# Edge softmax of a graph layer on one Trainium2 core: one pair of scans for two, and an accumulator cleared and added up by two engines

## What is computed

```python
alpha = einsum('ehc,hc->eh', leaky_relu(x_r[dst] + x_j, 0.2), att) + log(edge_attr)[:, None]   # 8 heads
amax  = segment_max(alpha, dst)
ex    = exp(alpha - amax[dst])
denom = segment_sum(ex, dst)
out   = segment_sum(x_j * (ex / denom[dst])[..., None], dst)
```

## Time and profile before

| what | time |
|---|---|
| median of the timed runs | 5361.09 us |
| span of the profiled execution (the profile gives no other time of it) | 5935.3 us |
| `normalise_edges`, first to last instruction of VectorE | 1488.2 to 1611.0 us |
| `aggregate_edges`, first to last instruction of VectorE | 1612.0 to 2075.7 us |
| last addition (L1109) | 13.74 us |

### The profile page before, as it was taken

How to read it: one execution, slowest core, us unless ns; L and a number is a source line. 1 busy time by engine, 2 the same in 40 slices (tenths; PEclk the granted TensorE clock), 3 DMA queues, 4 the chain that set the end, 5 groups by cost and what they waited for, 6 DMA issues and landing times. The chain is left out here.

```text
span 5935.3 us, 66919 instructions
## 1 busy us (share of the span) xinstructions
PE 3546.3 (60%) x13782; PEld 2710.2 (46%) x13783; DVE 2982.8 (50%) x6982; ACT 1018.9 (17%) x2146; POOL 3055.9 (51%) x2888
## 2 busy tenths in 40 slices
PE   4744455454389865998444544454445454466998
PEld 3633233232267654776433433333434444455666
DVE  5466566666899964445433333334333333354443
ACT  0111121121179801221000000000000000013121
POOL 1266677676368624221466666663666666612111
PEclk9877767776599976998566566655555555566999
DMA  4487666666578762223311111111111111123221
GB/s 108 136 217 211 202 207 203 204 206 195 158 227 271 224 188 88 63 63 97 106 28 28 29 28 28 29 29 32 28 29 28 28 29 28 29 62 98 70 87 37
DMA packets 432122, 617.01 MB, mean 104 GB/s; under 512 B 100329, under 2 KB 309161, under 8 KB 431721
## 3 DMA queue, kind: packets, MB, share of 16 engines
q1 hardware_dynamic: 304733, 389.03, 21.1%
q0 software_dynamic: 107440, 200.97, 14.1%
q10 hardware_dynamic: 19852, 25.94, 1.6%
HBM read 419.67 MB, written 209.64 MB: 106 GB/s over the span
## 5 line engine op out<-in xcount | busy, mean ns | idle before, releaser
L1857 POOL DMA_INDIRECT big<-t_d,src_tiles x1564 | 1483.7, 949 | 957.2 <-issue 450.8
L2080 PE MATMUL v_bank<-big,v_oh 128*128 x3328 | 716.2, 390 | 1216.6 <-issue 830.3
L2080 PEld LDWEIGHTS v_bank<-big,v_oh 128*128 128x128 f32 x3328 | 674.7, 300 | 1302.8 <-issue 1302.2
L653 POOL DMA_INDIRECT big<-xl_d,src_steps x832 | 859.8, 1033 | 378.1 <-issue 356.0
L1935 DVE TENSOR_TENSOR big<-big,v_bank 128x64 f32 x1664 | 366.5, 220 | 1285.3 <-DMA xj_d<-big 973.2
L759 PE MATMUL se_z_ps<-big,se_oht 128*128 x1664 | 608.7, 517 | 628.5 <-issue 385.9
L759 PEld LDWEIGHTS se_z_ps<-big,se_oht 128*128 128x128 f32 x1664 | 386.8, 250 | 850.4 <-issue 780.7
L692 DVE TENSOR_TENSOR se_z<-se_z_ps,big 128x528 f32<-128x528 f32 x416 | 291.4, 700 | 461.1 <-DMA es_ts<-src_p 256.8
L1122 PE MATMUL ae_bank<-ae_v,ae_oh 128*128 128x266 f32 x1664 | 402.3, 397 | 49.8 <-DVE big L1106 36.7
L1081 POOL TENSOR_TENSOR ae_v<-ae_v,ex 128x1792 f32<-128x1792 f32 x104 | 334.1, 3215 | 178.1 <-DMA ae_v<-xj_d 178.0
L1122 PEld LDWEIGHTS ae_bank<-ae_v,ae_oh 128*128 128x128 f32 x1664 | 310.4, 191 | 141.5 <-DVE big L1106 53.0
(11 more groups left out here) (468 smaller groups left out, 5316.9 us busy)
## 6 DMA issues: line engine op xcount, KB each, us to landing
xj_d<-big SPq DMA_DIRECT2D x208, 528.0 KB
ae_v<-xj_d SPq DMA_DIRECT2D x208, 528.0 KB
se_dlb<-dlr_d SPq DMA_DIRECT2D x104, 256.0 KB
big<-t_d,src_tiles POOLq DMA_INDIRECT x1564
buf_d<-ne_blank SPq DMA_DIRECT2D x4, 4112.0 KB
e_xs<-buf_d SPq DMA_DIRECT2D x106, 129.0 KB, 2.1
big<-xl_d,src_steps POOLq DMA_INDIRECT x832
cp_y<-y_d SPq DMA_DIRECT2D x14, 896.0 KB, 7.4
```

The lines of the kernel that those rows point to most:

```text
L653: nc.gpsimd.indirect_dma_start(half_of(u)[:, k, :], None, table, bass.IndirectOffsetOnAxis(ap=m.src[:, t:t + 1], axis=0)).then_inc(landed[ ...
L1857: nc.gpsimd.indirect_dma_start(rows[:, t % RING, :], None, table, bass.IndirectOffsetOnAxis(ap=m.srct[:, t:t + 1], axis=0)).then_inc(lande ...
L2080: last = nc.tensor.matmul(bank[u][:, k * MH:(k + 1) * MH], oh[:, u, k, :], of_block(rows, at[k]), start=True, stop=True)
```

## The change

In `normalise_edges`:

- One forward scan inside the chunks and one backward scan over its result, both without initial value. Both ends of every chunk (`cols`, now four columns) then go through one merge, in which forwards and backwards lie side by side in rows of 256.
- Columns that belong to the chunk's first or last segment get the neighbours' maximum by two masks: `off_first` = (key - first key) * -1e30 in `m.ex`, `off_last` = (last key - key) * -1e30 in `key`. ScalarE makes both in four passes over 6656 columns, between its copies for the folding. VectorE applies each with `max(top, mask + carry)` in four quarters, ahead of the subtraction.
- L867 is cut into four quarters by step; the scaling of `run` (L861) moves behind them.
- On TensorE the transposes move ahead of the second product of the folding; ScalarE, not VectorE, copies their 13 groups out of PSUM. Of the 13 groups on the way back ScalarE copies 7 (between its exponentials), VectorE 6.

In `aggregate_edges`:

- GpSimd clears `acc` before its first multiplication; VectorE clears `acc1` as its second instruction, ahead of L1092 of group 0.
- The last addition is shared: blocks 0 to 30 on VectorE, 31 to 48 on GpSimd.

The core of the diff:

```diff
@@ normalise_edges, VectorE
+                c.did(V.tensor_copy(cols[:, 1:2], key[:, 0:1]))
+                c.did(V.tensor_copy(cols[:, 2:3], key[:, CL - 1:CL]))
+                c.did(V.tensor_scalar(minus[:, :], key[:, 0:1], -1.0, None, ALU.mult))
...
-                V.tensor_tensor(top.rearrange(...), exv, lnw..., ALU.add).then_inc(s["logw"], 1)
-                for q in range(NQ4):
-                    dve.wait_ge(s["turned"], q + 1)
-                    V.tensor_copy(al[:, q * 512:(q + 1) * 512], bank[q % 4][:, :]).then_inc(s["back"], 1)
+                for q in range(4):
+                    j = slice(q * J4, (q + 1) * J4)
+                    V.tensor_tensor(turned_top[:, :, j, :], exv[:, :, j, :], wide[:, :, j, :], ALU.add).then_inc(s["logw"], 1)
+                dve.wait_ge(s["same"], 1)
+                c.did(V.tensor_scalar(run[:, 1:CL], run[:, 1:CL], -1.0, -MASKED, ALU.add, ALU.mult))
                 dve.wait_ge(s["back"], NQ4)
...
+                c.did(V.tensor_tensor_scan(top, run[:, 0:CL], al, MASKED, ALU.add, ALU.max))
+                c.sync()
+                c.did(V.tensor_tensor_scan(top[:, ::-1], run[:, 1:CL + 1][:, ::-1], top[:, ::-1], MASKED, ALU.add, ALU.max))
+                c.sync()
+                V.tensor_copy(cols[:, 0:1], top[:, CL - 1:CL]).then_inc(s["cols"], 1)
+                V.tensor_copy(cols[:, 3:4], top[:, 0:1]).then_inc(s["cols"], 1)
...             (one merge: six copies of a row, the operations of L903 to L918 on 256 columns)
+                c.did(V.tensor_copy(carry[:, :], bank[1][:, 0:2]))
+                dve.wait_ge(s["apart"], 4)
+                for q in range(4 + 2):
+                    if q < 4:
+                        V.scalar_tensor_tensor(top[:, o], off_first[:, o], carry[:, 0:1], top[:, o], ALU.add, ALU.max).then_inc(s["left"], 1)
+                    if 0 <= q - 1 < 4:
+                        dve.wait_ge(s["left"], q)
+                        V.scalar_tensor_tensor(top[:, o], off_last[:, o], carry[:, 1:2], top[:, o], ALU.add, ALU.max).then_inc(s["right"], 1)
+                    if 0 <= q - 2:
+                        dve.wait_ge(s["right"], q - 1)
+                        V.tensor_tensor(al[:, o], al[:, o], top[:, o], ALU.subtract).then_inc(s["exps"], 1)
+                for q in range(ON_ACT, NQ4):      # ON_ACT = 7, NQ4 = 13
                     dve.wait_ge(s["unturned"], q + 1)
+                    V.tensor_copy(*unturned_out(q)).then_inc(s["done_dve"], 1)
@@ ScalarE, behind a_back
+                for q in range(NQ4):
+                    act.wait_ge(s["turned"], q + 1)
+                    nc.scalar.copy(al[:, q * 512:(q + 1) * 512], bank[q % 4][:, :]).then_inc(s["back"], 1)
+                nc.scalar.activation(off_first, key, ACT.Identity, bias=minus[:, 0:1], scale=1.0).then_inc(s["apart"], 1)
                 (kv_back)
+                nc.scalar.mul(off_first, off_first, MASKED).then_inc(s["apart"], 1)
                 (t1_back)
+                nc.scalar.activation(off_last, key, ACT.Identity, bias=cols[:, 2:3], scale=-1.0).then_inc(s["apart"], 1)
                 (m0_back x3)
+                nc.scalar.mul(off_last, off_last, MASKED).then_inc(s["apart"], 1)
+                exps(0); exps(1); copy_out(0..2); exps(2); copy_out(3..5); exps(3); copy_out(6)
@@ aggregate_edges
+                nc.gpsimd.memset(acc[:, :, :], 0.0).then_inc(s["cleared"], 1)          # GpSimd, ahead of its loop
+                pool.wait_ge(s["added"], NS)
+                nc.gpsimd.tensor_tensor(acc[:, ON_DVE:NB, :], acc[:, ON_DVE:NB, :], acc1[:, ON_DVE:NB, :], ALU.add)
+                V.memset(acc1[:, :, :], 0.0).then_inc(s["cleared"], 1)                 # VectorE, ahead of its loop
-                        V.memset(acc[:, :, :], 0.0).then_inc(s["zeroed"], 1)
-                        V.memset(acc1[:, :, :], 0.0).then_inc(s["zeroed"], 1)
-                        dve.wait_ge(s["zeroed"], 3)
+                        dve.wait_ge(s["cleared"], 2)
-                V.tensor_tensor(acc[:, :, :], acc[:, :, :], acc1[:, :, :], ALU.add)
+                V.tensor_tensor(acc[:, 0:ON_DVE, :], acc[:, 0:ON_DVE, :], acc1[:, 0:ON_DVE, :], ALU.add)   # ON_DVE = 31
```

More of the change, by code:

```diff
@@ L776, in normalise_edges @@
         small, lnw, empty = sb("small", [P, NS]), sb("lnw", [P, NS]), sb("empty", [P, NS])
-        cols = sb("cols", [P, 4])
-        cki, carry = sb("cki", [P, 1]), sb("carry", [P, 2])
-        rows = sb("rows", [1, 6, P])
+        cols, minus = sb("cols", [P, 4]), sb("minus", [P, 1])
+        carry = sb("carry", [P, 2])
+        rows = sb("rows", [1, 7, 2 * P])
         bank = [ctx.enter_context(nc.psum_tensor(f"ne_bank{i}", [P, 512], F32)) for i in range(4)]
         blank = sb("blank", [P, 1, RW])
-        s = {n: m.sem("ne_" + n) for n in "blank blanked w ln logw turned back cols rowps rows colps exps exped unturned done chain".split()}
+        s = {n: m.sem("ne_" + n) for n in ("blank blanked w ln ends same logw turned back apart cols rowps rows colps left right exps exped unturned "
+                                         "done_act done_dve chain").split()}
         wfct, wq, wkt, wvt = (sb(n, [P, KC, D]) for n in ("wfct", "wq", "wkt", "wvt"))
@@ L866, in _ @@
                 c.sync()
[L867 to L872 removed]
+                wide = lnw[:, :].rearrange("p (c j) -> p c j", c=CH).unsqueeze(3).to_broadcast([P, CH, CS, H])
@@ L875, in _ @@
                 c.sync()
[L877 to L886, removed]
@@ L887, in _ @@
-                c.sync()
[L888 to L922, removed]
@@ new lines, in _ @@
+                V.tensor_copy(cols[:, 0:1], top[:, CL - 1:CL]).then_inc(s["cols"], 1)
+                V.tensor_copy(cols[:, 3:4], top[:, 0:1]).then_inc(s["cols"], 1)
+                VALUE, NEAR, FAR, JOINED, WHOLE, STATE, CARRIED = range(7)
+                hc = lambda r: rows[:, r, :].rearrange("a (h c) -> a h c", c=CH)
+                dve.wait_ge(s["rowps"], 1)
+                for r, backward, i in ((VALUE, 0, 0), (NEAR, 0, 1), (FAR, 0, 2), (VALUE, 1, 3), (NEAR, 1, 2), (FAR, 1, 1)):
+                    v = bank[0][0:1, i * P:(i + 1) * P].rearrange("a (c h) -> a h c", h=H)
+                    c.did(V.tensor_copy(hc(r)[:, backward * H:(backward + 1) * H, :], v[:, :, ::-1] if backward else v))
@@ new lines, in _ @@
+                c.sync()
+                c.did(V.tensor_tensor_scan(rows[:, STATE, :], rows[:, WHOLE, :], rows[:, VALUE, :], MASKED, ALU.add, ALU.max))
+                c.sync()
+                c.did(V.tensor_tensor(hc(CARRIED)[:, :, 1:CH], hc(STATE)[:, :, 0:CH - 1], hc(JOINED)[:, :, 1:CH], ALU.add))
+                c.sync()
+                for backward in range(2):
+                    v = rows[:, FAR, backward * P:(backward + 1) * P].rearrange("a (c h) -> a h c", h=H)
+                    V.tensor_copy(v[:, :, ::-1] if backward else v, hc(CARRIED)[:, backward * H:(backward + 1) * H, :]).then_inc(s["rows"], 1)
@@ L969, in _ @@
                 last.then_inc(s["a_made"], 1)
+                for q in range(NQ4):
+                    if q >= 4:
+                        pe.wait_ge(s["back"], q - 3)
+                    pe.wait_ge(s["logw"], (4 * q + 3) // J4 + 1)
+                    for i in range(4):
+                        last = nc.tensor.transpose(bank[q % 4][:, i * P:(i + 1) * P], top[:, (4 * q + i) * P:(4 * q + i + 1) * P], m.ident[:, :])
+                    last.then_inc(s["turned"], 1)
                 pe.wait_ge(s["a_back"], 1)
@@ L1036, in aggregate_edges @@
         U = 4
+        ON_DVE = 31
         def exps(g, k0, k1):
```

89 lines of the change are left out of this document (58 added, 31 removed).

## The result

The changed kernel takes 5311.84 us, the median of five launches (5305.04 to 5320.15), beside 5360.26 for the kernel before: ratio 0.9913, 95% interval 0.9903 to 0.9924, so 41 to 52 us less. The forecast was 5318 with a range of 5305 to 5335; the direction, the size and the range hold.

A forecast was written before the change was run, and what follows sets the result against it. VectorE's list was taken to set the end of both stages up to the loop, where VectorE and TensorE are both full. Normalising -31.3, clearing -15 and last addition +3.5 gave -42.8 us: 5318 from a median of 5361.1, range 5305 to 5335.

The forecast's parts named there:

- The first scan: Normalising, up to the first scan: it starts earlier in the stage, -12.8 us (bounds -10.0 and -14.5).
- Scans and merge: Normalising: two of four scans go, -28.1 us; one merge of double rows replaces two, -3.7 us.
- The eight new operations: Normalising: merged maxima applied by eight VectorE operations of 1664 columns, 1.82 us each, +14.6 us.
- After the subtraction: Normalising, the copies and exponentials up to the stage's end: 6.5 us for 7.8, -1.3 us (bounds -2 and +2).
- What has to stay hidden: Normalising: ScalarE's mask passes and GpSimd's operations finish before VectorE asks for the masks, with 5.6 us of cover.
- The first rival: Normalising: GpSimd misses the seam between the scans, so the last mask comes late: +7.4 us, 5325; chance 0.12.
- Clearing: Start of the aggregation: clears split over VectorE and GpSimd bring the first addition earlier, -15 us (bounds -10 and -22).
- The further 3 us that I set down for the second group: Aggregation's start: second group's additions wait behind L1092 of group 2 and GpSimd without its lead, taking back up to 3.
- The last addition: End of the aggregation: VectorE's and GpSimd's shares add up, 17.2 us for 13.7, +3.5 us (to +4.9).
- The second (side by side): End of the aggregation: both engines' parts of the last addition overlap, 8.5 us less, 5310; chance 0.08.
- The third (the loads give it back): Aggregation loop: loads pace it, so an earlier first addition gains nothing, 5333; chance 0.08.
- The fourth: Aggregation loop: L1092 falls elsewhere against GpSimd in each of 104 groups; slower, 5380 at +0.6 a group; chance 0.05.

The follow-up runs named there:

- Run 7: Changed kernel with TensorE's transposes back behind the second folding product; profile only: first scan starts 35.6 us into the stage for 26.9.
- run 8: Changed kernel with two further ScalarE passes over 6656 columns ahead of the last mask; profile only: VectorE waits 4.68 us.
- run 2: Kernel before with only the new aggregate_edges, normalise_edges left old: 5360.8 us, ratio 1.0002.
- run 4: Changed kernel with VectorE's part of the last addition replaced by a fill; profile only: GpSimd's part 10.3 us for 18.8.
- 3: Changed kernel with the last addition on VectorE alone: 5313.89 us, ratio 0.9934.
- 9: The changed kernel as it is, launched once more: 5312.61 us, ratio 0.9931.
- run 5: Changed kernel with both accumulators cleared on VectorE ahead of its loop, none on GpSimd: 5319.9 us, ratio 0.9935.
- run 11: Changed kernel with all eight multiplications of a group on GpSimd, last addition on VectorE alone, clears over three engines: 5305.16 us, ratio 0.9902.

## Why the prediction was right

The mechanism held in both stages, term by term. That the sum of the profiles comes out at 42.9 us for 42.8 forecast is luck: the stage in front gained 0.9 less than forecast, the clearing 2.6 more, and the last addition cost 1.6 more.

- *The first scan.* -12.8 forecast, -12.9 in the profile, and this is luck in part as well. TensorE stayed at half clock (granted 0.50) for 4.7 us of the transposes and not for the 2.6 of three groups; at full clock a group took 0.51 us and not 0.60, since the 0.60 that I had read from the way back holds VectorE's copies of 0.68, for which TensorE waited. The two errors cancel: first transpose to last copy, 9.2 us as forecast. Run 7 shows that TensorE's order is worth 8.7 of the 12.9; the rest is not taken apart.
- *Scans and merge.* -28.1 and -3.7 forecast; -27.8 (the 0.33 us by which the second scan is longer, at the seam with GpSimd) and -3.6.
- *The eight new operations.* +14.6 forecast, +14.9 measured (with the subtraction 22.2 for 21.8): each 1.86, not 1.82.
- *After the subtraction.* -1.3 forecast, -1.0.
- *What has to stay hidden.* 5.6 us of cover forecast, 6.9 in the profile, 6.8 by run 8 (11.5 us of further passes gave 4.7 of waiting). The first rival, GpSimd missing the seam, did not happen.
- *Clearing.* -15 forecast with bounds -10 and -22, -17.6 measured: 20.7 earlier, and 3 taken back, most of it in the first group. There TensorE works at half clock (granted 0.50), 0.88 us a step, and VectorE, with nothing stored up, waits 0.84 before the second addition and 0.45 before each of the next three, until the clock rises: the eight additions take 6.2 us for the 3.02 of the earlier trace rows. The further 3 us that I set down for the second group did not come here: the step 0 of group 2 took 0.45 us. In runs 2 and 4 it did come (3.13 and 3.40).
- *The last addition.* +3.5 forecast, +5.1 measured. The mechanism holds, the size was off: GpSimd's 4788 columns took 10.1 (10.3 beside a fill), not 8.4, above my bound of 9.9 too. I took the rate, 1.75 ns a column, from a multiplication whose second input repeats one number 32 times; two full inputs cost 2.1. That the repeated input is the reason is argued, since no run changes it alone. The estimate by the Trainium skill (GPSIMD Engine Reference, "Performance versus the Vector engine"), 10.5, was nearer, and the trace comes close to it: 10.1 us. My small price was wrong as well: 0.53 us was only what L823 had left behind the scan. By itself the same trace has 0.73 for 256 columns with two full inputs, and in proportion to that my bound would have been 13.6 us instead of 9.9:

```profile
1518.67 0.73 POOL L820 TENSOR_TENSOR kvt<-kvt,bd 128x256 f32<-128x256 f32 x1 [4.49 <-ACT kvt L944]
```

- *The rivals.* The second (side by side) is out by run 4. The third (the loads give it back) is out: the loop grew by 3, not 15. The fourth is real where I gave it 0.05: in its profiled launch the aggregation alone, behind the old stage, lost its whole gain to it. One launch of the changed kernel in eleven was at 5355, which may be the same and has no profile. My argument against it, that a load starts when group g-4 is summed and so the phase comes back within a few groups, named the right loop and the wrong sign: the same coupling holds the two engines together, for some ten groups in run 4 and some forty in run 2.

What decides whether a launch falls into it can be followed in the first groups. The changed kernel, run 2 and five more profiled runs (3, 4, 7, 8, 9) have the same code up to the last addition; in run 2 TensorE's first 30 matmul records took longer, as the timelines of the two show (changed kernel, then run 2):

```profile
1453.91 9.00 PE L1165 MATMUL ae_bank<-ae_v,ae_oh 128*128 128x266 f32 x30 [1.74 <-POOL ae_v L1122]
...
1460.18 0.45 DVE L1137 TENSOR_TENSOR ae_v<-ae_v,ex 128x256 f32<-128x256 f32 x1
```

```profile
1483.35 9.86 PE L1125 MATMUL ae_bank<-ae_v,ae_oh 128*128 128x266 f32 x30 [1.73 <-POOL ae_v L1082]
...
1490.11 3.13 DVE L1097 TENSOR_TENSOR ae_v<-ae_v,ex 128x256 f32<-128x256 f32 x1
```

In the one VectorE's step 0 of group 2 gets through in 0.45 us, in the other it begins 0.5 us later against the start of these records (6.76 us for 6.27) and sits a multiplication of GpSimd out. All seven profiles line up so. The clock below is TensorE's granted clock in the fifth microsecond behind the start of these records; in the first three it is 0.50 in every run, and from the seventh on 1.00:

| run | clock, 4 to 5 us | step 0 of group 2 begins after | it takes | loop |
|---|---|---|---|---|
| 8 | 1.00 | 6.05 us | 0.68 us | 414.9 us |
| 3 | 1.00 | 6.07 | 0.65 | 414.9 |
| changed kernel | 0.96 | 6.27 | 0.45 | 415.1 |
| 7 | 0.92 | 6.32 | 0.42 | 415.1 |
| 9 | 0.89 | 6.34 | 0.42 | 415.4 |
| 4 | 0.74 | 6.48 | 3.40 | 423.6 |
| 2 | 0.50 | 6.76 | 3.13 | 438.1 |

The later TensorE's clock rises to full in the first group, the later VectorE comes to step 0 of group 2, and between 6.34 and 6.48 us the loop tips over. That a late rise is the trigger is borne out by seven profiles without an exception, but no run moves the rise by itself. Nor is it explained why the rise came late in runs 2 and 4, or why the launches of run 2, behind the old stage, are strewn so much wider than those of the changed kernel.

## What to carry to other kernels

Before work is split between VectorE and GpSimd, look at how many of VectorE's inputs lie in SBUF: with two, the parts add up, and GpSimd's columns cost twice as much, so an addition was 13.7 us alone and 18.9 shared, while fills and additions from PSUM ran beside GpSimd freely. Where both engines alternate inside a loop, the loop can have more than one rhythm (415 or 424 to 438 us here), and a few tenths of a microsecond at its start go with the one or the other: price it from several launches, and look at the first groups of the loop. Look also at what a waiting engine's releaser waits for: TensorE stood behind a small GpSimd operation that VectorE had shut out. A block moved past such a wait can be worth as much as removed instructions (here 8.7 us from TensorE's order), provided that what it passes has cover; here the profile gave that cover to within a microsecond.

## What the runs showed of the hardware

- A fill of 13034 columns shows 10.92 us in the record and 2.66 of idleness before it, on VectorE; on GpSimd 10.96 and no such gap, from the stage's first moment. VectorE's real cost is the 13.59 together: with both clears on VectorE ahead of the loop (run 5) the first addition moved from 17.2 to 30.8 us.
- A fill of VectorE costs the same beside a fill of GpSimd as without: 10.92 + 2.66 in the changed kernel, 10.92 + 2.67 before. GpSimd's 10.96 was not measured by itself; 8778 columns took 7.41 in run 11, the same 0.84 ns a column.
- A waiting operation of GpSimd gets through between two adjacent long ones of VectorE even where it has 256 columns and two inputs: GpSimd ended 0.48 us after the second scan had begun, and that scan took 14.36 us for the 14.03 of the first. In all eleven profiles with the new first stage the second scan takes 14.36 to 14.37 us and GpSimd's operation ends within 0.6 us of its start. That the 0.33 us are the price of the seam is argued: no run has the scans without it.
